# The last step of an expert layer moved from GpSimd to VectorE, and the expert blocks' places in two engines' order laid anew

## The reference

```python
h = layernorm(x) * (1 + ca) + sa;  x = x + ga * causal_attention(h)      # 8 heads, low-rank keys and values
h = layernorm(x) * (1 + cb) + sb;  x = x + gb * moe_gelu(h)              # 8 experts of width 64, top 2
h = layernorm(x) * (1 + ca) + sa;  x = x + ga * mamba(h)                 # 256 channels, 16 states, scan over tokens
h = layernorm(x) * (1 + cb) + sb
combine = zeros((t, 8)).at[arange(t)[:, None], top_idx].add(softmax(top_w))
x = x + gb * (sum over e of combine[:, e] * (gelu(h @ w1[e] + b1[e]) @ w2[e] + b2[e]))   # width 512, top 2
```

## Time and profile before

| | us |
|---|---|
| median of 3 runs | 1442.75 (1438.37 to 1442.99) |
| the profiled execution | 1431.02 |
| its span, first to last instruction | 1429.2 |
| VectorE busy | 1006.9 (70%) |
| TensorE busy | 1073.9 (75%) |
| ScalarE busy | 755.0 (53%) |
| GpSimd busy | 661.1 (46%) |

### The profile page before, as it was taken

How to read it: one execution, slowest core, us unless ns; L and a number is a source line. 1 busy time by engine, 2 the same in 40 slices (tenths; PEclk the granted TensorE clock), 3 DMA queues, 4 the chain that set the end, 5 groups by cost and what they waited for, 6 DMA issues and landing times. The chain is left out here.

```text
span 1429.2 us, 19661 instructions
## 1 busy us (share of the span) xinstructions
PE 1073.9 (75%) x6224; PEld 728.4 (51%) x6224; DVE 1006.9 (70%) x2193; ACT 755.0 (53%) x1492; POOL 661.1 (46%) x466
## 2 busy tenths in 40 slices
PE   6864798687887788677886788767986877877282
PEld 4531265454564555555564555645564555644172
DVE  3868976598748976598757977588865986489301
ACT  3634364675547654575537754476546754466030
POOL 1006802397216842197315952088323972069602
PEclk9985599899898989989898989989897998879586
DMA  5103003350323313341223313252133503133252
GB/s 159 61 15 101 18 15 111 126 177 28 105 79 140 110 30 117 125 164 38 83 86 131 133 36 109 85 167 72 43 98 125 177 21 110 59 129 121 95 176 65
DMA packets 74151, 137.24 MB, mean 96 GB/s; under 512 B 10504, under 2 KB 44344, under 8 KB 73920
## 3 DMA queue, kind: packets, MB, share of 16 engines
q1 hardware_dynamic: 67936, 123.20, 26.3%
q0 software_dynamic: 5392, 12.59, 2.8%
q10 hardware_dynamic: 720, 0.19, 0.1%
HBM read 116.34 MB, written 15.42 MB: 92 GB/s over the span
## 5 line engine op out<-in xcount | busy, mean ns | idle before, releaser
L1675 DVE TENSOR_TENSOR_SCAN probs_T<-bank,probs_T 128x512 f32<-128x512 f32 x256 | 301.2, 1211 | 39.0 <-ACT bank L1256 28.6
L610 POOL TENSOR_TENSOR probs_T<-step_space,probs_T 128x1024 f32<-128x1024 f32 x120 | 281.8, 2355 | 18.8 <-DMA probs_T<-b_rows_dram 16.2
L1256 ACT ACTIVATE bank<-step_space,a_neg 128x512 f32<-128x512 f32 x256 | 170.0, 685 | 102.0 <-DVE probs_T L1675 83.9
L1190 ACT ACTIVATE probs<-bank,row_neg 128x128 f32<-128x128 f32 (+3 forms) x256 | 134.8, 529 | 146.5 <-DVE row_neg L1546 129.9
L894 PE MATMUL bank<-k_pad,q_lat 128*128 128x512 f32 (+3 forms) x512 | 188.7, 456 | 2.6 <-DMA k_pad<-xc 2.6
L1546 DVE TENSOR_REDUCE row_neg<-bank 128x1 f32<-128x128 f32 (+3 forms) x256 | 121.4, 485 | 80.1 <-PE bank L896 78.8
L858 PE MATMUL bank<-probs,w_ident 128*128 128x512 f32 x256 | 156.6, 697 | 9.1 <-DVE probs L1359 9.1
L629 POOL TENSOR_TENSOR step_space<-step_space,probs 128x512 f32<-128x512 f32 x112 | 142.2, 1269 | 40.4 <-DVE probs L1359 40.3
L1359 DVE TENSOR_TENSOR probs<-probs_T,bank 128x1024 f32<-128x1024 f32 x128 | 153.5, 1199 | 0.7 <-PE bank L858 0.3
L805 PEld LDWEIGHTS bank<-expert_w,hidden 128*128 128x128 f32 x960 | 130.3, 211 | 33.4 <-issue 32.9
L805 PE MATMUL bank<-expert_w,hidden 128*128 128x128 f32 x960 | 147.1, 301 | 0.0
(11 more groups left out here) (217 smaller groups left out, 1930.2 us busy)
## 6 DMA issues: line engine op xcount, KB each, us to landing
expert_w<-in_experts_dram SPq DMA_DIRECT2D x120, 512.0 KB, 3.4
probs_T<-b_rows_dram SPq DMA_DIRECT2D x64, 512.0 KB, 4.3
slots_in<-slots_dram SPq DMA_DIRECT2D x24, 256.0 KB, 3.3
results_dram<-slots_out SPq DMA_DIRECT2D x24, 256.0 KB, 4.1
k_pad<-xc SPq DMA_DIRECT2D x64, 64.0 KB, 2.0
x_in<-in_x_dram POOLq DMA_DIRECT2D x8, 256.0 KB, 3.3
gate<-gate_rows_dram SPq DMA_DIRECT2D x1, 2048.0 KB, 7.0
out_dram<-x_out POOLq DMA_DIRECT2D x7, 256.0 KB, 2.8
```

The lines of the kernel that those rows point to most:

```text
L610: ins = nc.gpsimd.tensor_tensor(inject[:, n % 3, :, :], u[:], row.unsqueeze(1).to_broadcast([P, DH, T]), ALU.mult)
L1190: f(probs_ring[:, n % 4, 0:(i + 1) * P], bank[SCORE_BANK[n % 4]][:, 0:(i + 1) * P], ACT.Exp, bias=row_neg[:, n % 4:n % 4 + 1], accum_out=r ...
L1256: f(decay(k)[:], delta[:, c, :], ACT.Exp, scale=a_neg[:, c, n:n + 1]).then_inc(dec_ok.sem, 1)
L1675: v.tensor_tensor_scan(state[:, n % 2, c, :], decay(DH * n + c)[:], inject[:, n % 3, c, :], 0.0, ALU.mult, ALU.add).then_inc(st_ok.sem, 1)
```

## The change

The four operations of `combine` go to VectorE, in two halves: the shares and the sum at the start of `iteration(b)` for batch `b - 2`, the gate and `x_mid` behind L1635. `shares` gets a second buffer. GpSimd's `store` moves behind `gate_weights`. The tables are new, the last quad's results are taken by ScalarE at unit 2 of the next `attend`, and at decay 31 a gelu is followed by no load of the decays' table.

```diff
-        shares = sb("shares", [P, 2, NT])
+        shares = sb("shares", [P, 2, 2, NT])
...
+            def end_experts(b):
+
+                save_slots(b, 1)
+                for n in SP_EXPERTS["end"]:
+                    fetch_expert(b, n)
+                for q in range(2, NQ):
+                    save_slots(b, q)
...
-                for q in SP_SAVES["end"]:
-                    save_slots(b - 1, q)
+                end_experts(b - 1)
...
-            def combine(b):
...
                 if b < B - 1:
                     load(b + 1)
-                if b >= 2:
-                    combine(b - 2)
-                    store(b - 2)
                 send_rows(b - 1)
                 gate_weights(b)
+                if b >= 2:
+                    store(b - 2)
                 sum_states(b)
             collect_rows(B - 2)
-            combine(B - 2)
+            send_rows(B - 1)
             store(B - 2)
-            send_rows(B - 1)
             collect_rows(B - 1)
...
+                    if n == RESULTS_UNIT and b >= 2:
+                        take_results(b - 2, NQ - 1)
...
                 early(0)
                 ln_modulate(b, 2, MISC)
+                early(1)
                 for c in range(2 * DH):
                     if c == DH:
-                        early(1)
+                        early(2)
                         nc.scalar.preload_act_table_set("silu_and_others")
...
+                early(3)
...
                             nc.scalar.preload_act_table_set("gelu_and_others")
                             pieces(b - 1, ACT_SCAN[k])
-                            nc.scalar.preload_act_table_set("natural_log_exp_and_others")
+                            if k < NS * DH - 1:
+                                nc.scalar.preload_act_table_set("natural_log_exp_and_others")
...
+            def combine(b, k):
+
+                if k == 0:
+                    dve.wait_ge(collected.sem, collected.at(b + 1, 0))
+                    tt(rows[:].rearrange("p k t d -> p (k t) d"), rows[:].rearrange("p k t d -> p (k t) d"),
+                       shares[:, b % 2, :, :].rearrange("p k t -> p (k t)").unsqueeze(2).to_broadcast([P, 2 * NT, P]),
+                       ALU.mult).then_inc(combined.sem, 1)
+                    dve.wait_ge(combined.sem, combined.at(b, 1))
+                    tt(rows[:, 0, :, :], rows[:, 0, :, :], rows[:, 1, :, :], ALU.add).then_inc(combined.sem, 1)
+                else:
+                    dve.wait_ge(combined.sem, combined.at(b, 2))
+                    dve.wait_ge(x_sent.sem, x_sent.before(b))
+                    tt(rows[:, 1, :, :], rows[:, 0, :, :], gate[:, b:b + 1, 3, :].to_broadcast([P, NT, P]), ALU.mult
+                       ).then_inc(combined.sem, 1)
+                    dve.wait_ge(combined.sem, combined.at(b, 3))
+                    tt(x_out[:], rows[:, 1, :, :], x_mids[b % 2][:], ALU.add).then_inc(combined.sem, 1)
...
             def iteration(b, behind):
                 mark, link, check = linker(dve, chain, b)
 
+                if b >= 2:
+                    combine(b - 2, 0)
                 choose(b, 0, link)
...
                 tt(x[:], x[:], gated_bias[:].to_broadcast([P, NT, P]), ALU.add).then_inc(bias_added.sem, 1)
+                if b >= 2:
+                    combine(b - 2, 1)
...
-PE_EARLY = (_fills(0, 3) + _done(0) + _fills(3, _upto(2)) + _done(1) + _fills(_upto(2), _upto(3)),
+PE_EARLY = (_fills(0, 4) + _done(0),
...
-SP_SAVES = {1: (0,), 5: (1,), "end": (2, 3)}
+SP_SAVES = {2: (0,)}
```

59 lines of the change are left out of this document (22 added, 37 removed).

## The result

The changed kernel takes 1336.95 us (median of 4 runs, 1335.34 to 1339.31); the kernel before took 1440.56 beside it. The ratio is 0.9285, 95% interval 0.9255 to 0.9315.

The account below looks back on a forecast made before the run. VectorE was taken to bound the scan; elsewhere a chain through TensorE, ScalarE and VectorE. Gains of 11.4 us a batch in five batches (57) plus the rest made 72: 1431.0 to 1359, plus 11.7 gave 1371, range 1345 to 1405.

Parts of the forecast that it names:

- the exclusion: Attention: GpSimd's combination and VectorE exclude each other; moving the combination off GpSimd gains 6.0 us a batch, ends 3.7 and 6.6.
- only the exclusion goes: Rival: the new places move waits and net to nothing, leaving the combination's gain in the attention; 1414 us, 10%.
- the gather comes late: Rival: the last results, copied into the next attention, are gathered too late for `choose`; 1401 us with 5 over, 3%.
- The arrival on VectorE: Combination's 2.1 and 1.4 us on VectorE hide in waits for router and convolution; cost 0, ends 0 and 0.7.
- Fewer pieces ahead of the transposes: Before the convolution: two blocks and a result leave TensorE's way to the transposes; gains 2.7 us a batch, ends 2.0 and 3.2.
- Results 0: Convolution to projections: their copy leaves ScalarE's chain and goes behind the logarithms; gains 1.1 us, ends 0 and 1.6.
- Results 14 at state 15: Scan's end: the result moves in front of the first scores; costs 1.0 us a batch, ends 0.5 and 2.
- The scan: Waits for decays give 4.1 us a batch, two low-clock stalls take 1.8; net gain 2.3, ends -2 and 4.1.
- a scan that stays low: Rival: TensorE stays at the low clock of 0.50 and the scan grows by 21 us; 1515 us, 3%.
- The sum over batches: Whole run: -57 us for batches 2 to 6, -5.9 batch 1, -8 batch 7, -1 tail; together -72.
- The distance to the median: Whole run: median of the runs lies 11.7 us above the profiled execution, added to 1359 to forecast 1371.
- all controls reached: Rival: the best ends of the terms come together, -16.2 us a batch; 1342 us, 12%.

Follow-up runs that it names:

- comb_only: Kernel before with the old places of the expert pieces and only the combination moved to VectorE; 1413.87 us, ratio 0.9803.
- early_take: order_only with results 14 back at state 14, its gelu behind decay 28, and the last quad's results copied behind decay 31; 1393.25 us, ratio 0.9681.
- order_only: Changed kernel's new places of the pieces, with the combination left on GpSimd at the attention's start; 1340.53 us, ratio 0.9306.
- ahead: Changed kernel with block 2, results 1 and block 3 back ahead of the transposes of the convolution's layernorm; 1365.16 us, ratio 0.9467.
- res0: Changed kernel with ScalarE's copy of the first four results ahead of the silu table load again, results 3 ahead of block 4; 1364.58 us, ratio 0.9454.
- r14: Changed kernel with results 14 back at state 14, its gelu behind decay 28 and none behind the last decay; 1364.73 us, ratio 0.9472.
- before_again: The kernel before, unchanged, timed and profiled once more; 1443.56 us, ratio 1.0032.
- late_take: Kernel before with only the last quad's results copied at unit 2 of the next attention instead of behind decay 31; 1404.94 us, ratio 0.9780.
- both_old: Kernel before on the old places with the edits of late_take and comb_only together; 1409.45 us, ratio 0.9747.
- after_again: The changed kernel, unchanged, run once more; 1343.54 us, ratio 0.9293.
- pool_later: Changed kernel with the combination on GpSimd, placed behind the gating of the weights; 1339.57 us, ratio 0.9297.
- g9w: g9s plus unused TensorE products in the pause at state 0 of the scan; 1328.85 us, ratio 0.9202.
- g9s: Changed kernel with a gelu group moved from decay 8 to 9 and eight unused TensorE products ahead of the small layer's transposes; 1329.58 us, ratio 0.9210.

## Why the prediction was right or wrong

Of the 34 us, 22 are the sum: -72 forecast, -94.0 measured from span to span. The other 12 are the distance from the profiled execution to the median. The steps that failed are two. The 11.7 us between the profile and the median of the kernel before were added to the sum, as if the changed kernel would have them too. It has none: its profiled executions took 1336.96 and 1346.49 us, at medians of 1336.95 and 1343.54. And terms of the sum were too small, most of all the one from convolution to projections, put at 0.9 us a batch (1.1 less 0.2) and measured at 1.7 to 3.2. A third error, which of the two edits ends the meeting of the engines, did not move the number; it stands under the exclusion.

| us gained | forecast, a batch | measured, mean of 2 to 5 | forecast, batches 1 to 6 | measured |
|---|---|---|---|---|
| attention | 6.0, less 1.0 for results 14 | 5.7 | 25.0 | 28.5 |
| clock in the small layer | 0.5 | 1.3 | 2.5 | 6.5 |
| to the convolution | 2.7 | 3.3 | 16.2 | 19.7 |
| to the projections | 1.1, less 0.2 | 1.7 | 5.4 | 12.2 |
| from there to the scan | none | 0.0 | 0.0 | 1.8 |
| scan | 2.3 | 1.8 | 13.8 | 12.1 |
| sum | 11.4 | 13.8 | 62.9 | 80.8 |

**The exclusion: right in size, wrong in owner.** Forecast 6.0 with ends 3.7 and 6.6; on the old places the attention went from 54.9 to 48.2 us, 6.7, with either cure. The rival "only the exclusion goes" had 1414, and comb_only measured 1413.87; that is partly luck, since the attention gave more than the rival's 5.0 a batch and the clock in other stages took some back. The term had no row for what lies beyond the 3.6 us of standstill; it was taken from a comparison of batches, and the rest goes with the clock of 0.65 behind the standstill, which is back whenever the standstill is (early_take) and gone without it. But the prediction gave the term to the combination's move alone. By it order_only would be some 30 us slower than the change, and it is within the measurement of it. The prediction had seen that the copy of the last results comes later, and read it as a danger only (the gather comes late). The same delay takes the combination out of VectorE's work on SBUF. To find it, the start of GpSimd's product had to be shifted by 3 us in the rows and held against what VectorE does then.

**The arrival on VectorE: right.** Forecast 2.1 and 1.4 us of work at a cost of 0; it took 2.3 and 2.6, and both pairs end inside a wait. Where the new operations meet GpSimd's gating, both sides grow, as the prediction allowed:

```profile
681.13 1.64 POOL L623 TENSOR_TENSOR gated_out<-w_out_w,gate 128x256 f32<-128x256 f32 x1 [5.54 <-DVE xn L1399]
```

```profile
699.94 1.80 POOL L623 TENSOR_TENSOR gated_proj<-w_wprojT,gate 128x512 f32<-128x512 f32 x1 [16.04 <-DVE xn L1399]
```

`gated_out` began 0.17 us behind VectorE's product by the shares and takes 1.64 us, against 0.73 in order_only. VectorE's addition (L1362), begun while `gated_out` ran, takes 1.10 us, and its product by the gate (L1366), begun 0.57 us behind `gated_proj`, takes 1.78; in the tail, where GpSimd gates nothing, they take 0.69 each.

**Fewer pieces ahead of the transposes: right mechanism, a little small.** 2.7 forecast, 3.3 measured, and 3.3 once more when ahead undid it. The give-back by the block that stands between transposes and L1012 was not there: TensorE does it while ScalarE makes `hT`.

**Results 0: too small.** 1.1 forecast with an end at 1.6, 1.7 measured here. In batches 1, 6 and 7 of the first profile the gain was 2.1 to 3.2, and res0 costs 3.7 (with results 3 also moved ahead of block 4, so it is not the old arrangement either). The term counted the 0.60 of the copy and part of a wait of 2.13 us; in res0, where TensorE does results 3 just ahead of the copy, that wait is 3.13. The old stretch was not one length, 10.4 us in batches 2 to 5 but 11.9 in batch 1 and 11.5 in batch 7, and is 8.7 in every batch now; the prediction read it in batch 4 alone.

**Results 14 at state 15: the size fits, but it buys something.** 1.0 us was added, and the attention of the new places is 49.2 us against 48.2 of the old ones without the exclusion. That results 14 makes this difference isn't shown: r14 has them back at state 14, and its attention is 50.0. What the prediction called free, the gelu with its own load behind the last decay, is worth more than that: with it back in the group behind decay 28 (r14), scan and attention are 3.4 us longer in each batch. r14 is not the old arrangement, whose last group stood behind decay 25, so this is the price of the group and not the gain of the change.

**The scan: near, by two errors that cancel in part.** 2.3 forecast, as 4.1 less 1.8 for two stalls, and 1.8 measured. The decays' waits fell from 28.6 to 8.0 us, 2.9 a batch, and one stall of 1.3 for TensorE's broadcast came, at the low clock, as foreseen:

```profile
728.07 0.61 PE L1036 MATMUL bank<-split,select 96*128 96x512 bf16 x1 [8.73 <-DVE probs L1351]
...
734.57 0.38 PE L1036 MATMUL bank<-split,select 96*128 96x512 bf16 x1
```

0.61 us is the low level and 0.38 the full one; between them run results 4, quad 2 and results 5, and the two blocks of state 2 come behind, at the full level. The rival of a scan that stays low did not come near: 0.86.

**The sum over batches: too small at the edges.** Batch 1 was put at 5.9 and batch 7 at 8. Their own stages gave 9.0 and 14.0, and batch 6, counted like the others, 16.4. That is 14 us more than forecast; the four batches between are 10 more, the tail 1, and the start of the run gave 3 back. Batch 1 was given the terms of batch 4 without the attention and the clock, and what they missed is mainly the longer stretch to the projections, 3.2 instead of 0.9. Batch 7 had no sum of its own: its attention alone gave 4.4, its way to the convolution 3.2 and to the projections 2.7. Batches 6 and 7 held one more stretch at the low clock, from the projections to the scan (10.2 us against 8.4).

**The distance to the median: carried over without a reason.** That stretch is a part of the other 12 us. In before_again, whose profiled execution (1440.37) is near the median, it is 10.2 in four of seven batches. The projections' products there:

```profile
765.38 3.78 PE L1037 MATMUL bank<-proj,w_dt_w 112*128 112x512 f32 x4 [0.78 <-ACT proj L1241]
```

and in the profile on which the prediction rests:

```profile
759.71 1.99 PE L1037 MATMUL bank<-proj,w_dt_w 112*128 112x512 f32 x4 [0.78 <-ACT proj L1241]
```

The granted clock of the 12 us around them is 0.72 in the one and 1.00 in the other. So the profile of before was one of the shorter executions of its kernel (its runs go from 1428.4 at a mean clock of 0.884 to 1451.7 at 0.860). Of the 9.4 us between the two profiles of before, this stretch has 3.6 and the one ahead of it, from convolution to projections, 4.6. The changed kernel has 8.4 and 8.7 us in these two in every batch from 1 on, in both its profiles: where the kernel before varied, it does not. This goes with the new places: comb_only, late_take and both_old have 10.2 in five or six batches, and no kernel with the new places has it in a batch from 1 on. Which of the places does it isn't shown; ahead, res0 and r14 undo one each, and none brings it back. What the changed kernel's two profiles differ by lies ahead of batch 1. after_again's profile is 9.5 us longer than the first, and all of it is there before batch 0's scan begins (131.9 against 122.2 us); the batches behind it are alike to 0.2 us.

The best case, all controls reached at 1342 with 12%, was nearest, in part by luck. Its terms are too large (81 us for five batches, against 71.8 measured in batches 2 to 6), and it carried the same distance of 12 us, which is not there; the two errors cancel.

## What to carry to other kernels

When an operation stands still beside another engine's, ask for its start before asking for its place: a delay of 3 us by two lines was worth as much as moving the work, and the two do not add. A group of work in a foreign mode, here gelus between two table loads, hid here if everything it needed was ready when it began, so its inputs belong one step earlier and the straggler behind the last deadline. A term read in one batch should be read in all of them before it is multiplied: the stretch to the projections had 10.4 us in four batches and up to 11.9 in the others. And before a profile's distance to the median is carried over, look into which stretches it lies, and whether the change touches them.

## What was not expected of the hardware

- GpSimd's product of SBUF tensors lets VectorE's reductions and copies out of PSUM run at full speed (1.36 us for two row maxima), and holds an operation on 4 columns for 1.68 us instead of 0.15 and, in pool_later, two `TENSOR_SCALAR` of 512 columns for 2.23 us in all.
- It holds both ways: VectorE's 512-column product takes 1.78 us beside GpSimd's `gated_proj` and 0.69 alone, GpSimd's `gated_out` 1.64 and 0.73.
- A standstill costs more than itself: 3.6 us of it went with 6.7 us of attention, in which the granted clock then fell to 0.65 over ten microseconds.
- The meeting is exact: where VectorE's operation begins 0.23 us behind GpSimd's and 0.24 us in early_take, the rows are the same 1.68 and 3.23 us.
- A higher mean clock is not a shorter time: the profiled executions of g9w and g9s have 0.927 and 0.897, and take 1331.4 and 1331.2 us.
